# New instruction orders for an audio tower kernel, and other batches in its sorted group

## The chip, the cores and the metric

The kernel runs on one core of a Trainium2 chip. The metric is the device time of one execution in microseconds; the time shown is the median of three. One execution was also recorded by the hardware profiler, and all rows below come from it. A core has a matrix engine (TensorE, PE in the profile), VectorE (DVE), ScalarE (ACT), GpSimd (POOL) and SyncE (SP), which here issues DMAs. Each engine takes its own instructions strictly in order and waits on semaphores that others raise.

## The reference

The input is 8 batches of 375 rows of 128 numbers, all in float32. Each batch passes through three parts:

```python
# token part
h = silu(conv1(x));  h = silu(conv3(h));  h = conv1(h)          # 128 -> 64 -> 64 -> 128
y = layer_norm(h + x);  y = layer_norm(gelu(y @ wf1) @ wf2 + y)
h = max over 3 neighbouring rows of y                            # 373 rows are left
# attention part
n = layernorm(h);  q = (n @ Wq + bq) * s;  k = n @ Wk + bk
h = h + softmax(q @ k.T) @ n
# mixture of 8 experts, the two best of each row
n = layernorm(h);  w = top-2 gates of softmax(relu(n @ gw1) @ gw2)
h = h + sum over e of w[e] * (gelu(n @ we1[e] + be1[e]) @ we2[e] + be2[e])
```

## The kernel before

Batches go through the parts one by one or in pairs. Every step has a short name and a number, and each engine's order is written out by hand as a list of such names (lines 55 to 118). The lists are walked by five loops (TensorE at line 956, VectorE 671, ScalarE 513, GpSimd 440, SyncE 366), so the place of a name in a list is the place of its instructions in that engine's queue. In TensorE's list the number behind the colon is the PSUM bank (one of eight) that the step writes; `claim` (line 939) makes the step wait until the last reader of that bank is done. ScalarE and VectorE share the evacuation of PSUM: a name such as `b1` or `pt0` may stand in either list, and the engine in whose list it stands does the copy. Names that also stand in TensorE's list are there the matrix step, and in the other lists what follows it.

The steps, in the order in which data pass them:

- `a1` to `a7`: the token part. `a1` and `a2` are convolutions, each followed by a tanh and an affine copy on ScalarE (1.15 us together) and a product on VectorE. `a3` is the third convolution; VectorE adds the input and takes the statistics of a layer norm. `p1` on GpSimd turns these into a scale (lines 444, 446, and 451 and 453 when the norm is applied by ScalarE), `l1` applies it, `a4` transposes. `a5` and `a6` are the feed-forward part, `p2` and `l2` its norm, `a7` the transposition, `mp` the maximum over three rows.
- `hr`, `p3`, `l3`, `b1`, `bq`, `bk`, `sc0` to `sc2`, `pt0` to `pt2`, `at`: the attention of one batch. VectorE's `sc` is the row maximum, ScalarE's the exponential.
- `p4`, `l4`, `h1`: the norm ahead of the experts and its transposition into `x32`. `g1`, `g2`, `g3` are the gates of a pair of batches.
- Four batches are dense: every expert is computed for every row. `D1.n` is half of a first layer (two matmul instructions at line 1110), `dg` its GELU on ScalarE (line 621), `D2` the second layer (twelve instructions at line 1117), `da` the weighted sum on VectorE (line 871), `ct` and `bd` the biases of the second layers.
- Four batches are sorted: `rk` and `cnt` rank the rows by expert, `scat` (24 indirect DMAs on GpSimd, line 469) writes rows into a sorted buffer in DRAM, `lx` (SyncE) and `lw` (GpSimd, line 479) load 19 blocks of 256 rows and the weights of each block's expert, `T`, `L1`, `L2` on TensorE (lines 1126, 1134, 1143) with `xT`, `gl`, `yv` compute them, `st` stores them, `gat` (24 indirect DMAs, line 491) gathers each row's two results, and `fin` (lines 927 and 931) adds them. Of the sorted buffer's tables (`cnt` on VectorE) every block is known only after the last of the four batches is ranked, and no gather starts before the last block is stored.
- `out` and `od` on SyncE store the results of sorted and dense batches.

Before the change batches 0, 1, 4, 5 are sorted and 2, 3, 6, 7 dense. `GROUPS` (line 25) says so; the number of `D1`, `D2`, `da` counts along the list of dense batches, eight experts each, so that `D1.0` to `D1.31` are batches 2 and 3.

Of the kernel before, what the change touches and what calls it, by code (L numbers as in the profile page):

```python
# [60 lines left out]
sc0.3:0 sc1.3:6 sc2.3:7 at.2:5 hr.4:6 g2.0:0 pt0.3:7 pt1.3:1 pt2.3:2 a4.6:3 a4.7:7 at.3:1 hr.5:3 h1.2:0 a5.3:7
D1.0:0 D1.1:6 b1.4:1 D1.2:2 bq.4:1 bk.4:3 D1.3:5 h1.3:4 D1.4:3 g1.1:4 g2.1:4 sc0.4:1 sc1.4:4 sc2.4:7 rk.0:0
b1.5:6 a6.6:2 bq.5:6 bk.5:0 a6.7:3 sc0.5:0 sc1.5:1 sc2.5:4 pt0.4:7 pt1.4:6 pt2.4:5 D1.5:7 at.4:6 ct.0:0 ct.1:5
pt0.5:4 pt1.5:1 pt2.5:0 bd.0:4 at.5:0 D2.0:4 D1.6:7 D1.7:5 h1.4:6 D2.1:0 D2.2:5 a7.6:2 D2.3:4 h1.5:2 D1.8:0
a7.7:3 g1.2:2 D1.9:4 D1.10:3 g2.2:2 D1.11:0 hr.6:3 D2.4:4 D1.12:3 D1.13:0 D1.14:2 D1.15:5 D2.5:6 D2.6:0 D2.7:5
rk.2:2 cnt.0:3 b1.6:7 D1.16:1 bq.6:7 bk.6:1 D1.17:2 D1.18:1 D1.19:2 D1.20:1 D1.21:2 sc0.6:7 sc1.6:2 sc2.6:4
hr.7:1 bd.1:6 D2.8:3 D1.22:1 D1.23:7 D2.9:2 D2.10:4 D1.24:5 D1.25:7 D1.26:3 D1.27:5 D2.11:2 D1.28:4 D1.29:5
b1.7:3 pt0.6:4 pt1.6:2 pt2.6:5 bq.7:4 at.6:5 T.0:4 bk.7:2 L1.0:4 T.1:3 D2.12:7 L2.0:3 L1.1:2 T.2:3 T.3:7 sc0.7:4
sc1.7:5 L2.1:2 h1.6:7 L1.2:3 T.4:7 L1.3:2 L2.2:3 L1.4:7 L2.3:3 sc2.7:2 L2.4:3 T.5:7 T.6:1 D2.13:0 L1.5:1 T.7:2
pt0.7:5 pt1.7:0 L1.6:3 pt2.7:0 D1.30:5 T.8:2 D1.31:0 D2.14:7 L2.5:3 L2.6:5 L1.7:3 T.9:5 L1.8:0 L2.7:3 T.10:5  # L70
# [1119 lines left out]
```

## Time and profile before

| | us |
|---|---|
| median of 3 runs | 287.95 (287.29 to 288.83) |
| the profiled execution's own time | 289.53 |
| its span, first to last instruction | 287.7 |
| TensorE busy | 248.6 (86%) |
| VectorE busy | 156.2 (54%) |
| ScalarE busy | 160.7 (56%) |
| GpSimd busy | 130.7 (45%) |
| mean granted TensorE clock | 0.955 |

The span is what the trace covers; the execution's own time is 1.8 us longer. An engine is busy while it works on an instruction, not while it waits on a semaphore. The granted clock is 1.0 where TensorE runs at 2.4 GHz and 0.5 where it runs at 1.2 GHz.

### The profile page before, as it was taken

The numbers are of one execution on the slowest core, as the hardware profiler recorded it, in microseconds if no ns is written. First come the engines' busy times: TensorE is split into PE (matmuls) and PEld (weight loads), VectorE is DVE, ScalarE is ACT, GpSimd is POOL, SyncE is SP. The second block draws the span as 40 slices with busy tenths as digits, with TensorE's granted clock in tenths as the row PEclk, the third lists the DMA queues.
The fourth block names the chain that finished last, engine by engine and source line by source line (L and its number), as shares of the span: only waits on it lengthen the run. The fifth ranks groups of instructions, "written<-read, shape, count | busy, mean of one in ns | idle before, by whom it ended". The sixth has DMA issues, their size and how long they took to land.

```text
span 287.7 us, 5162 instructions
## 1 busy us (share of the span) xinstructions
PE 248.6 (86%) x1484; PEld 191.6 (67%) x1484; DVE 156.2 (54%) x646; ACT 160.7 (56%) x333; POOL 130.7 (45%) x225
## 2 busy tenths in 40 slices
...
PEclk9986977999999999995999999999999999999898
...
GB/s 123 186 162 271 326 405 295 0 0 2 1 2 0 2 2 21 45 36 10 0 2 30 48 63 260 245 208 160 186 190 232 26 75 39 45 80 68 66 49 53
DMA packets 22318, 28.87 MB, mean 100 GB/s; under 512 B 5791, under 2 KB 18532, under 8 KB 22292
## 3 DMA queue, kind: packets, MB, share of 16 engines
...
q10 hardware_dynamic: 576, 0.10, 0.2%
q14 instruction: 14, 0.11, 0.1%
...
## 4 chain that ended last, share of the span: by engine, by line
PE 43%; POOL 22%; issue 15%; DVE 7%; DMA 5%; ACT 3%; POOLq 2%; ACTq 1%; DVEq 0%
POOL xs L469 10%; POOL yg L491 9%; PE PS L1143 6%; PE PS L1134 5%; PE PS L970 4%; PE PS L1117 4%; PE PS L1055 3%; PE PS L1037 3%; DMA wm_p<-in_wm 3%; PE PS L1110 3%; PE PS L949 2%; POOL rstd L446 2%; PE PS L1006 2%; PE PS L1007 2%; PE PS L986 2%
## 5 line engine op out<-in xcount | busy, mean ns | idle before, releaser
L621 ACT ACTIVATE gd<-PS,bias 128x373 f32<-128x373 f32 x64 | 35.6, 573 | 29.7 <-PE PS L1110 28.4
L1117 PEld LDWEIGHTS PS<-w_all,gd 128*125 128x125 f32 x384 | 48.5, 201 | 3.8 <-issue 0.6
L1117 PE MATMUL PS<-w_all,gd 128*125 128x128 f32 x384 | 49.4, 286 | 0.0
L1110 PE MATMUL PS<-xt_sb,w_all 128*128 128x373 f32 x128 | 47.0, 488 | 2.7 <-DVE x_sb L871 2.4
L491 POOL DMA_INDIRECT yg<-ys,pos_y x24 | 29.2, 1217 | 25.7 <-issue 25.7
L469 POOL DMA_INDIRECT xs<-xn,pos_x x24 | 28.8, 1199 | 18.6 <-DVE pos_x L844 12.0
L871 DVE SCALAR_TENSOR_TENSOR x_sb<-PS,comb,x_sb 125x128 f32<-125x128 f32 x84 | 24.2, 344 | 20.8 <-PE PS L1117 20.0
L444 POOL TENSOR_TENSOR ve<-mv,eps 125x3 f32<-125x3 f32 x32 | 7.6, 238 | 57.7 <-DVE mv L654 57.6
L1110 PEld LDWEIGHTS PS<-xt_sb,w_all 128*128 128x128 f32 x128 | 21.8, 190 | 14.4 <-issue 6.0
L446 POOL TENSOR_TENSOR rstd<-ve,mhalf 125x3 f32<-125x3 f32 x32 | 27.5, 860 | 2.5
L479 POOL DMA_DIRECT2D blk_w<-w_all x19 | 10.5, 552 | 32.6 <-issue 23.1
L633 ACT ACTIVATE gb_t<-PS,blk_w 128x256 f32<-128x256 f32 x38 | 15.8, 470 | 11.3 <-PE PS L1134 11.2
L1143 PEld LDWEIGHTS PS<-blk_w,gb_t 128*128 128x128 f32 x152 | 18.4, 191 | 3.7 <-ACT gb_t L633 2.6
L1143 PE MATMUL PS<-blk_w,gb_t 128*128 128x128 f32 x152 | 20.3, 280 | 0.5 <-ACT gb_t L633 0.4
L1134 PE MATMUL PS<-xb_t,blk_w 128*128 128x256 f32 x76 | 19.5, 383 | 0.0
L917 DVE TENSOR_TENSOR yblk<-PS,blk_w 128x256 f32<-128x256 f32 x19 | 8.0, 423 | 19.6 <-PE PS L1143 19.4
L1055 PEld LDWEIGHTS PS<-xn,prob_t 125*125 125x125 f32 (+1 forms) x144 | 16.7, 187 | 2.6 <-issue 2.2
L1055 PE MATMUL PS<-xn,prob_t 125*125 125x129 f32 (+1 forms) x144 | 17.7, 276 | 0.7 <-ACT prob_t L594 0.3
L970 PE MATMUL PS<-hc,wm_p 128*128 128x375 f32 x24 | 11.9, 649 | 5.8 <-DMA wm_p<-in_wm 4.9
L1037 PE MATMUL PS<-k_t,q_t 128*125 128x373 f32 x48 | 16.8, 483 | 0.1
L949 PE MATMUL PS<-ident,xn 124*128 124x124 f32 (+1 forms) x48 | 8.4, 289 | 8.0 <-ACT xn L509 7.5
L1134 PEld LDWEIGHTS PS<-xb_t,blk_w 128*128 128x128 f32 x76 | 13.1, 190 | 2.5 <-ACT xb_t L626 0.7
...
## 6 DMA issues: line engine op xcount, KB each, us to landing
...
```

What stands on the lines that cost most here:

```text
L446: pool.tensor_tensor(rstd[i][:, n % 2, :], ve[i][:, n % 2, :], mhalf[:], ALU.pow)\
L469: pool.indirect_dma_start(xs[g], bass.IndirectOffsetOnAxis(ap=pos_x[:, b // 2, s, i:i + 1], axis=0), xn4[:, b % XN4, j, :], None).then_inc ...
L491: pool.indirect_dma_start(yg[:, m % 2, s, j, :], None, ys[g], bass.IndirectOffsetOnAxis(ap=pos_y[:, b // 2, s, i:i + 1], axis=0))\
L621: act.activation(gd[:, k % GD, c, 0:TP], of("D1", n)[:, 0:TP], ACT.Gelu, bias=bias128[:, 2 + k % E * HC + c:3 + k % E * HC + c]).then_inc( ...
L871: last = dve.scalar_tensor_tensor(flat(dst)[j], flat(of("D2", n)[0:P, :])[j], w[:, j, b % 2, e:e + 1], flat(h2[:, b, :])[j], ALU.mult, ALU ...
L970: last = pe.matmul(f[:, 0:T], wm_p[:, k, :], hc1[:, k:k + T], start=(k == 0), stop=(k == 2))
L1037: pe.matmul(f[0:P, 0:TP], q_t[:, s, OFF[j]:OFF[j] + P], k_t[:, s, :], start=True, stop=True)\
L1055: last = pe.matmul(f[0:P, j * (D + 1):(j + 1) * (D + 1)], prob_t[0:ROWS[c], s, c, OFF[j]:OFF[j] + P], xn3[0:ROWS[c], s, c, :], start=(c == ...
L1110: pe.matmul(f[:, 0:TP], w_all[:, k % E, c * 128:(c + 1) * 128], x32[:, DENSE[k // E], 0:TP], start=True, stop=True).then_inc(S["D1"], 1)
L1117: last = pe.matmul(f[0:P, j * D:(j + 1) * D], gd[:, n % GD, c, OFF[j]:OFF[j] + P], w_all[:, n % E, H + c * D:H + (c + 1) * D], start=(c == ...
L1134: last = pe.matmul(f[:, c * BLK:(c + 1) * BLK], blk_w[i][:, c * 128:(c + 1) * 128], xb_t[n % 2][:], start=True, stop=True)
L1143: last = pe.matmul(f[:, t * D:(t + 1) * D], gb_t[n % 2][:, c, t * 128:(t + 1) * 128], blk_w[i][:, H + c * D:H + (c + 1) * D], start=(c == ...
```

## The change

All instructions stay; their orders in the five lists change, TensorE's steps get other banks, and 56 evacuation steps change between ScalarE and VectorE. The sorted batches become 2, 3, 4, 5, the dense ones 0, 1, 6, 7, so `D1.0` to `D1.31` now belong to batches 0 and 1, and `rk.1` and `cw.0` replace `rk.0` and `cw.1`. ScalarE's list goes from 238 to 228 steps, VectorE's from 170 to 180: VectorE takes over five `l1`, three each of `a4`, `l3`, `bk` and `h1`, four `b1`, one `l4`; ScalarE takes over six `a7`, three `bq` and three `pt`, all net. The diff, cut to the places that the prediction speaks of:

```diff
-GROUPS = ((0, 1, 4, 5),)
+GROUPS = ((2, 3, 4, 5),)
...
 PE_ORDER = """
-a1.0:0 a2.0:0 a3.0:0 a1.1:1 a3.1:2 a1.2:2 a2.1:0 bf.0:2 a4.0:1 a2.2:3 a4.1:0 a3.2:1 a1.3:2 a3.3:3 a5.0:0 a6.0:0
-a6.1:3 a4.2:2 a3.4:1 a3.5:4 a4.3:5 a7.0:0 a7.1:3 a5.1:5 a4.4:3 a6.2:5 hr.0:3 hr.1:0 a4.5:4 a6.3:1 a5.2:4 a2.3:0
...
-T.17:7 L1.16:1 D1.35:7 D1.36:3 T.18:2 D1.37:0 L1.17:4 L2.16:2 L1.18:7 L2.17:4 ct.2:3 L2.18:7 ct.3:0 bd.2:3
...
+a1.0:0 a2.0:0 a1.1:1 a3.0:0 a3.1:1 a2.1:2 bf.0:1 a4.0:0 a1.2:3 a1.3:2 a4.1:0 a3.2:1 a3.3:3 a5.0:0 a2.2:2 a6.0:3
+a6.1:2 a4.2:0 a3.4:1 a3.5:4 a4.3:5 a2.3:6 a7.0:3 a7.1:2 a5.1:0 a4.4:2 hr.0:0 hr.1:2 a6.2:6 a6.3:2 a4.5:0 a3.6:3
+a3.7:5 a5.2:0 b1.0:4 bq.0:4 bk.0:3 b1.1:0 a7.2:6 a6.4:1 sc0.0:3 sc1.0:6 sc2.0:2 bq.1:5 bk.1:0 a7.3:4 a6.5:7
...
+pt2.5:1 D1.8:4 D1.9:3 at.5:7 h1.4:4 hr.7:3 D2.4:2 D1.10:4 D1.11:7 D1.12:3 D1.13:4 D1.14:7 D1.15:3 h1.5:4 D2.5:7
...
+L1.17:3 L1.18:4 g2.3:7 L2.17:3 L2.18:4 D2.15:3 D1.32:4 D1.33:7 D1.34:0 D1.35:1 D1.36:5 D1.37:4 ct.2:7 ct.3:0
...
 DVE_ORDER = """
-a1.0 a2.0 a3.0 a3.1 a1.1 a1.2 bf.0 a4.0 a2.1 a3.2 a3.3 a2.2 a6.0 a6.1 a3.4 a3.5 a7.0 a7.1 mp.0 a1.3 a6.2 hr.0
...
-yv.16 yv.17 yv.18 bd.2 da.16 da.17 da.18 da.19 da.20 fin.0 da.21 da.22 da.23 bd.3 fin.1 da.24 da.25 da.26 fin.2
-da.27 da.28 da.29 fin.3 da.30 da.31
+a1.0 a2.0 a1.1 a3.0 a3.1 l1.0 bf.0 l1.1 a2.1 a1.2 a3.2 a3.3 a1.3 a2.2 a6.0 a6.1 a3.4 a3.5 a4.2 a4.3 l1.4 mp.0
...
+yv.12 yv.13 yv.14 yv.15 yv.16 g2.3 yv.17 yv.18 g3.3 cw.3 da.15 bd.2 da.16 bd.3 da.17 da.18 fin.0 da.19 da.20
+da.21 fin.1 da.22 da.23 da.24 da.25 fin.2 da.26 da.27 da.28 fin.3 da.29 da.30 da.31
...
 POOL_ORDER = """
-p4.0 p3.2 p4.1 p3.3 p1.6 p1.7 p4.2 p3.4 p4.3 p3.5 scat.0 scat.1 scat.2 scat.3 scat.4 scat.5 scat.6 scat.7 scat.8
-scat.9 scat.10 p4.4 scat.11 p2.6 p4.5 p2.7 p3.6 scat.12 scat.13 scat.14 scat.15 scat.16 scat.17 scat.18 scat.19
-scat.20 scat.21 scat.22 scat.23 p3.7 lw.0 lw.1 lw.2 lw.3 lw.4 lw.5 p4.6 lw.6 lw.7 lw.8 lw.9 lw.10 lw.11 lw.12
...
+p2.4 p2.5 p4.0 p3.2 p4.1 p2.6 p2.7 p3.3 p4.2 p3.4 p4.3 p3.5 p4.4 scat.0 scat.1 scat.2 scat.3 p4.5 scat.4 scat.5
+scat.6 scat.7 scat.8 scat.9 scat.10 scat.11 p3.6 p3.7 scat.12 scat.13 scat.14 scat.15 scat.16 scat.17 scat.18
+scat.19 scat.20 scat.21 scat.22 scat.23 lw.0 lw.1 lw.2 lw.3 p4.6 p4.7 lw.4 lw.5 lw.6 lw.7 lw.8 lw.9 lw.10 lw.11
```

## Rows read from the trace of the kernel before

**Rows 1.** The page: the span, and the granted clock in 40 slices
```profile
span 287.7 us, 5162 instructions
PEclk9986977999999999995999999999999999999898
```

**Rows 2.** Busy time in stretches: stretch and length, then each engine, PEclk, DMA, GB/s
```profile
16.40:125.20 108.80, 96.80 (x570) 71.71 (x570) 80.69 (x344) 74.92 (x160) 51.47 (x106) 0.94 0.29 100
125.20:135.60 10.40, 6.58 (x33) 6.24 (x32) 2.78 (x9) 5.09 (x12) 7.67 (x16) 0.67 0.08 20
180.00:190.00 10.00, 9.53 (x62) 7.74 (x61) 3.42 (x9) 5.39 (x15) 3.15 (x7) 1.00 0.71 240
177.20:236.30 59.10, 58.57 (x388) 48.95 (x387) 22.49 (x91) 36.41 (x83) 10.96 (x22) 1.00 0.50 173
236.30:281.60 45.30, 41.61 (x259) 33.77 (x256) 22.05 (x75) 15.37 (x27) 29.21 (x24) 0.96 0.23 59
```

**Rows 3.** Timeline of the first 40 us: start, length, engine, instruction, idle before
```profile
11.19 4.09 PE L970 MATMUL PS<-hc,wm_p 128*128 128x375 f32 x6 [4.94 <-DMA wm_p<-in_wm]
18.36 0.85 PE L962 MATMUL PS<-xt_sb,wc_p 128*64 128x375 f32 x4
...
23.30 3.51 PE L970 MATMUL PS<-hc,wm_p 128*128 128x375 f32 x6 [0.26 <-DVE hc L688]
33.76 1.28 ACT L559 ACT_TABLE_LOAD   x1 [0.55 <-PE PS L999]
35.77 0.46 PE L1006 MATMUL PS<-wf_p,f 128*125 128x128 f32 x2 [2.10 <-ACT f L559]
```

**Rows 4.** Timeline of TensorE, 44 to 57 us
```profile
44.60 0.51 PE L949 MATMUL PS<-ident,n 125*128 125x125 f32 x3 [1.57 <-ACT n L509]
...
56.70 0.88 PE L949 MATMUL PS<-ident,xn 125*128 125x125 f32 x6
```

**Rows 5.** The chain of waits: start, length, what (two full-rate stretches)
```profile
137.36 0.63 PE PS L1110 x2
...
199.21 1.31 PE PS L1117 x12
```

**Rows 6.** Instruction groups by form: busy, mean ns of one, idle before
```profile
L662 DVE TENSOR_SCALAR xn<-h,mv,rstd 125x128 f32<-125x128 f32 x6 | 1.7, 342 | 0.0
L746 DVE TENSOR_SCALAR y_t<-PS,cols 128x375 f32<-128x375 f32 x6 | 3.9, 664 | 2.3 <-PE PS L949 2.3
L766 DVE TENSOR_SCALAR q_t<-PS,bias 128x373 f32<-128x373 f32 x6 | 3.6, 605 | 2.6 <-PE PS L1027 1.5 <-DVE w_top L847 0.7 <-DVE mv L654 0.4
```

**Rows 7.** Timeline of ScalarE, 61 to 64 us
```profile
61.94 1.28 ACT L588 ACT_TABLE_LOAD   x1
63.24 1.03 ACT L588 ACTIVATE prob<-PS,nmax 125x373 f32<-125x373 f32 x2
```

**Rows 8.** Timeline of several engines, 124 to 131 us
```profile
124.84 0.31 DVE L654 BATCH_NORM_AGGREGATE mv<-stat 125x2 f32<-125x6 f32 x3
...
126.52 0.89 POOL L446 TENSOR_TENSOR rstd<-ve,mhalf 125x3 f32<-125x3 f32 x1
...
128.05 1.26 ACT L509 ACTIVATE xn<-x_sb,nmr,rstd 125x128 f32<-125x128 f32 x3 [5.35 <-POOL nmr L453]
...
129.37 0.88 PE L949 MATMUL PS<-ident,xn 125*128 125x125 f32 x3 [3.83 <-ACT xn L509]
```

**Rows 9.** Timeline of TensorE at 172 us, and of POOL and SP before it
```profile
168.13 1.19 POOL L469 DMA_INDIRECT xs<-xn,pos_x  x1 [0.30 <-issue]
172.43 9.70 SPq L376 DMA_DIRECT2D blk_x<-xs  x7
...
172.50 0.54 PE L949 MATMUL PS<-ident,xn 125*128 125x125 f32 x3 [1.64 <-ACT xn L509]
```

**Rows 10.** Timeline of TensorE at 264 us
```profile
264.22 2.07 PE L1110 MATMUL PS<-xt_sb,w_all 128*128 128x373 f32 x4 [2.38 <-DVE x_sb L871]
...
277.50 2.79 PE L1117 MATMUL PS<-w_all,gd 128*125 128x128 f32 x24
```

**Rows 11.** The chain of waits, last 52 us: start, length, what
```profile
236.30 0.44 DVE yblk L917
...
239.53 1.29 POOL yg L491
...
274.55 3.47 DMA yg<-ys,pos_y
278.04 0.89 DVE acc L927 x3
```

More of the change, by code:

```diff
@@ L61 @@
[L61 to L70, printed above, removed]
@@ new lines @@
+at.1:2 hr.3:7 a7.4:6 a7.5:1 a6.6:0 h1.0:4 a6.7:6 b1.2:2 D1.0:4 D1.1:7 D1.2:1 h1.1:3 bq.2:2 bk.2:4 g1.0:7 D1.3:2
+sc0.2:4 sc1.2:7 b1.3:2 sc2.2:1 g2.0:0 bq.3:2 bk.3:3 a7.6:0 D1.4:2 sc0.3:3 sc1.3:0 pt0.2:1 pt1.2:7 pt2.2:4
+sc2.3:5 D1.5:7 at.2:4 pt0.3:5 hr.4:6 pt1.3:0 pt2.3:3 ct.0:5 ct.1:1 a7.7:0 at.3:3 bd.0:1 bd.1:0 h1.2:6 hr.5:5
+D2.0:4 b1.4:5 D2.1:2 bq.4:5 h1.3:7 bk.4:3 D1.6:5 g1.1:1 sc0.4:3 sc1.4:4 b1.5:2 g2.1:1 sc2.4:5 bq.5:2 bk.5:3
+D1.7:4 pt0.4:5 sc0.5:3 sc1.5:2 sc2.5:5 pt1.4:1 pt2.4:0 D2.2:7 at.4:1 rk.1:3 hr.6:7 D2.3:2 pt0.5:5 pt1.5:0
```

67 lines of the change are left out of this document (35 added, 32 removed).

## The prediction
> **What bounds the kernel now.** I read the page first, then busy time by stretches, then the timeline around each idle stretch of TensorE, and the chain of waits for the end. TensorE is the engine to follow: from 177 to 236 us it is busy 58.6 of 59.1 us [rows 2]. Its work at full rate is fixed: a `D1` takes 0.63 us and a `D2` 1.31 us [rows 5], so 0.11 us for one small matmul instruction. Only four things can move the span: idle time of TensorE, its half-rate stretches, what is placed behind the last sorted block, and the fixed end. The reader is to see these stalls:
> - In the head TensorE waits for weights until 11.2 us, then for ScalarE and VectorE between convolutions (11.2, 23.3, 35.8) [rows 3], then for layer norms (44.6) [rows 4]. The clock row shows reduced slices there [rows 1].
> - At 125.5 TensorE stands 3.8 us for batch 4's norm: its statistics were ready at 125.15, but GpSimd was inside a row of `scat` and got to the power at 126.5, ScalarE to `l4` at 128.05 [rows 8]. Behind the stall the granted clock is low, 0.67 over 10.4 us, and twelve `D2` instructions take twice 1.31 us. A clock at 1.2 instead of 2.4 GHz over some 6 us makes about 2.7 us more.
> - At 170.9 it stands 1.6 us for batch 7's `l3` [rows 9], whose `p3` is queued behind the last `scat`.
> - At 261.8 it stands 2.4 us for a bank that `da` frees late [rows 10], because VectorE sat in a `fin`; again the half rate follows (four `D1` instructions in 2.07 us).
> The end is two chains side by side. `L2.18` ends at 236.3; store, 24 gathers and their landing bring `fin.3` at 278.0 [rows 11], which is 41.7 us later, then 1.8 us for `fin.3`, 1.8 us for two `da`, and 6.1 us to store: 51.4 us, 287.7. TensorE's last `D2` ends at 280.3 [rows 10], 44 us behind `L2.18`.
>
> **The change part by part,** as shifts of the end of `L2.18` (236.3), and then the end.
>
> *A, what stands ahead of `L2.18`.* Before, 38 `D1` and 16 `D2` and one `ct` stand ahead; after, 32, 15 and none. 6 x 0.63 + 1.31 + 0.33 = 5.4 us earlier. This costs TensorE nothing in total and lets the gathers start earlier: -5.4.
>
> *B, the head.* `a1.1` moves ahead of `a3.0`. It now runs right behind `a2.0` (ends 15.3) and its tanh and copy (1.15 us) follow at 16.4 instead of 19.3; VectorE's product is done near 18.3, and `a2.1` can start at about 19.3 instead of 23.3. `a1.2`, `a1.3` and `a2.2` now fill waits of ScalarE on `a4.0` and `a5.0`. `a5.0` has its table load of 1.28 us and GELU [rows 3] behind it in both orders; following every step by the durations above I get `a6.0` near 31.3 instead of 35.8, with the same steps ahead of it in both lists. Then `a2.3` (2.0 us) is moved ahead of `a7.0`, where it covers the norms' waits [rows 4], and `a4.2`, `a4.3` on VectorE let `a5.1` go. Continued to `b1.0`, I get 48 instead of 56.7 us with equal work ahead. The hand count has no semaphore hops and may not see a lost clock stretch. I take -7.0; bounds -9 (the hand count) and -2 (only half of the first gain survives). The inputs of batches 6 and 7 are needed 4 us sooner; the `xb` steps on them ran before 27.7 us, so they are in by then.
>
> *C, the middle, until VectorE has batch 5's statistics.* This is at 125.2 before. Ahead of `at.5` TensorE gets four `D2`, four `D1`, two `a7`, `bd.1` and `hr.6` more: 5.2 + 2.5 + 0.7 + 0.7 + 0.3 = 9.4 us. They are not new work, they come from later, and fill waits; with B the same point is 125.2 + 9.4 - 7.0 = 127.6. But VectorE's load grows: between 16.4 and 125.2 it is busy 80.7 of 108.8 us, 74% [rows 2]. It gains ahead of this point five `l1`, three `l3`, one `l4` (0.87 each, from three at 0.342 that overlap), `l2` twice, four `a4` (0.66), `bk`, `bq`, `h1`, `b1`, `pt` (0.55 to 0.61), `mp.3`, four `da` (0.9), `bd.1`, `hr.6`: 25.7 us, and gives away five `a7`, three `bq`, five `pt`, `l2`, `l4`, `l3`, `a4`: 11.4 us (sizes from [rows 6]). So 95.0 us of work in 111.2 us, 85%. It can hold that only if it seldom waits, so I add 3.0 us of new stalls; bounds 0 and 10 (where it would be 78%). ScalarE has four more table loads here, at `sc0.2`, `sc0.4`, `sc0.5` and the returns to `dg`: 5.1 us, less 2.8 us of steps given away, 77 us of 74.9 before: it is not last. C: +3.0.
>
> A page bears on the table loads. The row shows 1.28 us and the exponential 0.02 us behind it [rows 7]. The Trainium skill, "ScalarE: Activation LUTs", section "What ACT_TABLE_LOAD costs", says that a drain of about 1.38 us comes on top, 2.66 us a switch. By that rule the four switches would cost ScalarE 10.6 us instead of 5.1, and C would be nearer its upper bound; the row contradicts it here, so nothing is taken from it.
>
> *D, the stall at 125.5.* `p4.4` now stands ahead of `scat.0` and `p4.5` behind only four `scat`, and `h1.4` has `hr.6`, `pt.5`, `D1.8`, `D1.9` and `at.5` between it and `at.4`. The norm's 3.8 us wait goes, and the 2.7 us of half rate with it: -6.6. What is late next is `rk.2` and, right behind it on VectorE, `l3.6`, `l3.7` and `b1.6`, where TensorE has only `cnt`, `D1.23` and `D2.9` as cover: some 0.5 us each for four places, +2.0; bounds 0 and 6.6 (another stall with its own slow clock). D: -4.6.
>
> *E, the stall at 170.9.* `p3.7` now goes ahead of `scat.12`: -1.6, with a short wait for a copy, -1.8 in all. The price of that place: 12 `scat` start one power later. Is the sorted stage then late? `scat` at 1.5 us each: 12 from `rk.2`'s positions take 18 us, the last lands 4.3 us after its start, then `lx.0` (before: 168.1 to 172.4 [rows 9], and 2.4 us to land). Behind `rk.2` the new list has 25.7 us of TensorE work ahead of `T.0`, against 2 + 16.5 + 4.3 + 2.4 = 25.2 us of this chain. It is just covered, with nothing left over.
>
> *F, the sorted stage.* Before, nineteen blocks share 59 us with 25 other steps; after, with six others, they take 40.7 us of work, 2.0 us a block. `L1.n+1` mostly has the bank of `L1.n`, so it waits for the two GELUs (2 x 0.47): 0.87 + 1.05 = 1.9 us a round, under 2.0. `lw` takes 1.7 us of GpSimd each; `p4.6` and `p4.7` stand ahead of `lw.4` and hold it until about 5 us behind `T.0`, where `L1.4` comes 10 us behind. The traffic is 577 KB a block (weights, rows in, rows out by the declared shapes), 2.4 us at the 240 GB/s of the densest stretch [rows 2], with six slots of prefetch. I take +1.5; bounds 0 and +7 (19 blocks at 2.4).
>
> *G, the end.* `fin.3` now has three `da` behind it instead of two: 41.7 + 1.8 + 2.8 + 6.1 = 52.4 us, +1.0; bounds 0 and 3. TensorE's own chain there is 32 x 0.63 + 17 x 1.31 + 2 = 44.5 us, with 7.4 us of `da` and store 51.9: as long. The wait at 261.8 goes, since `D2.25` and `D2.28` have a `da` of slack. SyncE's `od.1` behind `st.18` is ready before it is due.
>
> Sum: 236.3 - 5.4 - 7.0 + 3.0 - 4.6 - 1.8 + 1.5 = 222.0; + 52.4 = 274.4 us of span. The profiled execution took 289.53 for a span of 287.7, and the median is 1.6 us below it: 274.4 + 1.8 - 1.6, about 274.6. A difference under 0.5% (1.4 us) can't be told from no change.
>
> **The rivals.**
> *Sorted stage bound by transfers and GELU rounds.* For it: GB/s 240 while only six blocks are prefetched [rows 2], and hardly any filler is left. Against it: the stage before moved 173 GB/s with TensorE 99% busy, and needs 250 now. At 2.4 us a block it costs 5.5 us over my F: 280.
>
> *VectorE becomes the bound of the middle, and the kernel slower.* Place: 16.4 us to batch 5's statistics. If VectorE's busy share stays at 74% with 95.0 us of work, the point is at 16.4 + 128 = 144.4, 16.8 us behind 127.6 instead of 3; that is a span of 288.2, and with one half-rate stretch as in [rows 2] 291. It decides from a share of 74.6%: below it the change loses. For it: every norm, maximum and copy in its list is in order, and a norm there waits for GpSimd's power. Against it: before, VectorE mostly waited for TensorE, not the reverse; by hand it is 92% busy as far as `at.1`.
>
> *It does not change anything.* If head and middle keep their idle time and only A works, TensorE's last `D2` still ends at 280 and the gain is hidden beside it: 286 to 288.
>
> **How the numbers follow.** Forecast 0.60 (its own range 268 to 279); transfers 0.18 (278 to 284); no change 0.10; VectorE 0.12 (287 to 294). The range 267 to 286 leaves out about 0.05 below and 0.14 above. Faster 0.83, same 0.07, slower 0.10.
>
> **What would show it.** Right: `a2.1` starts near 19.3, `a6.0` near 31 to 33, `b1.0` by 51; no TensorE wait of over 2 us between 60 and 180; `L2.18` ends near 222 and `fin.3` starts 41.7 us later; VectorE's share to batch 5's statistics is over 80%. Wrong: a share of 75% or less there; GpSimd waiting with `scat` for positions beyond 2 us after `rk`; blocks 2.3 us apart; a new slice of low clock past 60 us.

## The result, and the profile after

| | before | after |
|---|---|---|
| median of 4 runs, same chip, us | 288.39 (287.29 to 289.76) | 265.21 (263.95 to 270.33) |
| ratio, 95% interval | | 0.918 (0.912 to 0.924) |
| the profiled execution's own time, us | 289.53 | 265.61 |
| its span, us | 287.7 | 263.7 |
| TensorE busy | 248.6 | 240.9 |
| mean granted clock | 0.955 | 0.976 |

The kernel became 8.2% faster, about 23 us. The forecast was 274.6 with a range from 267 to 286: the direction was right, and the time lies below the range. One of the four executions behind 265.21, the one of 270.33, was a slow one: the ratios here and below leave such executions out, the medians keep them.

The page of the changed kernel, which answers to [rows 1]:

```profile
span 263.7 us, 5144 instructions
...
PEclk9996797999999999999999999999999999999998
```

The clock is reduced only in the head and at the very end; the slice with 5 in the middle of [rows 1] has no counterpart.

Busy time in stretches, which answers to [rows 2] (same columns). The first line ends where VectorE has the statistics of batch 5, the next two are the stretch between two blocks of attention and the sorted stage, then the densest ten microseconds of its traffic and the end:

```profile
16.40:123.10 106.70, 101.00 (x637) 77.47 (x636) 92.95 (x390) 77.12 (x157) 43.68 (x95) 0.95 0.28 97
139.00:167.10 28.10, 25.94 (x161) 20.00 (x161) 18.83 (x65) 13.79 (x24) 16.90 (x17) 1.00 0.32 97
167.10:211.60 44.50, 44.50 (x300) 38.84 (x299) 12.27 (x41) 25.66 (x66) 10.66 (x21) 1.00 0.61 209
170.00:180.00 10.00, 10.00 (x70) 8.40 (x69) 2.91 (x9) 6.68 (x19) 3.06 (x5) 1.00 0.73 243
211.60:258.40 46.80, 45.77 (x287) 36.02 (x285) 25.47 (x104) 20.08 (x37) 29.24 (x24) 1.00 0.25 64
```

VectorE did 92.95 us of work in 106.7 us, a share of 87% where it had 74%, and the point came at 123.1 where it had been at 125.2, although TensorE had 9.4 us more ahead of it. In the sorted stage TensorE is busy in all of the 44.5 us, and its blocks come 2.1 us apart (`T.0` at 167.1, `T.18` at 205.1).

The head of the changed kernel, from the timelines of TensorE and ScalarE, which answers to [rows 3] and [rows 4]:

```profile
9.54 0.97 PE L970 MATMUL PS<-hc,wm_p 128*128 128x375 f32 x1 [3.10 <-DMA wm_p<-in_wm]
...
17.42 0.80 PE L970 MATMUL PS<-hc,wm_p 128*128 128x375 f32 x2
...
29.72 1.28 ACT L559 ACT_TABLE_LOAD   x1 [2.02 <-PE PS L999]
31.01 0.57 ACT L559 ACTIVATE f<-PS,bias 128x375 f32<-128x375 f32 x1
...
31.64 0.48 PE L1006 MATMUL PS<-wf_p,f 128*125 128x128 f32 x2
...
50.41 0.43 PE L949 MATMUL PS<-ident,xn 125*128 125x125 f32 x2
```

`a2.1` starts at 17.4 (before 23.3), `a6.0` at 31.6 (35.8), `b1.0` at 50.4 (56.7).

TensorE's waits in the changed kernel between 60 and 180 us (line, what it waited for: sum, number, longest), all of them:

```profile
PE PS L1037 <- DVE x_sb L871: 2.1, 2, 1.4
```

They are at `sc1.6` and `sc2.6`, whose banks a `da` still reads. The stalls of [rows 8] and [rows 9] are gone: `h1.4` runs at 120.7 without a wait, and while GpSimd works on the next norm's power (124.15) TensorE has dense steps (it is busy 10.32 of the 10.4 us from 123.1):

```profile
120.70 0.48 PE L949 MATMUL PS<-ident,xn 125*128 125x125 f32 x3
...
122.78 0.32 DVE L654 BATCH_NORM_AGGREGATE mv<-stat 125x2 f32<-125x6 f32 x3
124.15 0.89 POOL L446 TENSOR_TENSOR rstd<-ve,mhalf 125x3 f32<-125x3 f32 x1
...
126.92 0.54 PE L949 MATMUL PS<-ident,xn 125*128 125x125 f32 x3
```

The chain of waits of the changed kernel, its shares and its end; it answers to [rows 11]:

```profile
PE 83%; SPq 5%; DVE 4%; DMA 3%; issue 2%; ACT 1%; another core or an unknown queue 0%; DVEq 0%
...
209.74 1.88 PE PS L1143 x16
211.62 1.32 PE PS L1117 x12
...
254.42 3.96 PE PS L1117 x36
258.38 0.02 issue
258.40 0.35 DVE ob L871
```

`L2.18` ends at 211.6 instead of 236.3. The chain is TensorE's own from there on, and no longer that of the gathers; the two are nearly equally long, as VectorE's timeline shows. The last gather lands 41.8 us behind `L2.18` (before 41.7), and the last `da` starts 5 us later, after waiting 0.45 us for TensorE:

```profile
253.37 0.88 DVE L927 SCALAR_TENSOR_TENSOR acc<-yg,w_top,x_sb 125x128 f32<-125x128 f32 x3 [1.84 <-DMA yg<-ys,pos_y]
...
258.40 0.87 DVE L871 SCALAR_TENSOR_TENSOR ob<-PS,comb,x_sb 125x128 f32<-125x128 f32 x3 [0.45 <-PE PS L1117]
```

**Where the 24.7 us at `L2.18` came from.** For a step of TensorE, call its delay its start less the time that all steps listed ahead of it take at full rate. Between two steps the delay grows by TensorE's waits, by what half rate costs, and by short gaps between matmuls that the profile counts as busy (the 2.8 us of the sorted stage below are such gaps: the clock is 1.00 there and no wait is shown). So kernels with different orders can be compared. The table compares one profile with one profile, and its row B holds what the head's clock happened to be in each.

| stretch | step of the sum | delay grows before | after | forecast change | measured change |
|---|---|---|---|---|---|
| work ahead of `L2.18` | A | | | -5.4 | -5.4 |
| start to `b1.0` | B | 29.0 | 23.0 | -7.0 | -6.0 |
| `b1.0` to `at.5` | C | 8.6 | 2.9 | +3.0 | -5.7 |
| `at.5` to `b1.6` | D | 7.2 | 1.2 | -4.6 | -6.0 |
| `b1.6` to `T.0` | E | 4.2 | 3.0 | -1.8 | -1.2 |
| `T.0` to `L2.18` | F | 3.1 | 2.8 | +1.5 | -0.3 |
| sum | | | | -14.3 | -24.6 |
| `L2.18` to the end | G | 51.4 | 52.1 | +1.0 | +0.7 |

A's figure is the same in both columns because it is counted and not measured. Of the 10.4 us between forecast and result at `L2.18`, 8.7 are in C.

### The profile page after: what moved, and what is told of

The parts are those of the page before. It is cut to its first block, busy times and chain, and to the rows that moved or that the text cites. A ratio compares the mean times of both kernels' runs of the same rounds, so it can differ in the third digit from the quotient of the medians.

```text
span 263.7 us, 5144 instructions
## 1 busy us (share of the span) xinstructions
PE 240.9 (91%) x1484; PEld 186.6 (71%) x1484; DVE 163.3 (62%) x671; ACT 151.2 (57%) x307; POOL 126.2 (48%) x207
## 4 chain that ended last, share of the span: by engine, by line
PE 83%; SPq 5%; DVE 4%; DMA 3%; issue 2%; ACT 1%; another core or an unknown queue 0%; DVEq 0%
PE PS L1117 16%; PE PS L1110 14%; PE PS L1143 7%; PE PS L1134 7%; PE PS L1055 6%; PE PS L1037 5%; PE PS L949 4%; DMA xt_sb<-in_xt 3%; PE PS L1044 3%; PE PS L1006 2%; PE PS L1007 2%; PE PS L1027 2%; PE PS L1031 2%; PE PS L986 2%; SPq L330 2%
## 5 line engine op out<-in xcount | busy, mean ns | idle before, releaser
L1110 PE MATMUL PS<-xt_sb,w_all 128*128 128x373 f32 x128 | 45.7, 485 | 0.7 <-DVE x_sb L871 0.6
L1117 PEld LDWEIGHTS PS<-w_all,gd 128*125 128x125 f32 x384 | 44.4, 187 | 2.5
L1117 PE MATMUL PS<-w_all,gd 128*125 128x128 f32 x384 | 45.8, 273 | 0.0
L444 POOL TENSOR_TENSOR ve<-mv,eps 125x3 f32<-125x3 f32 x32 | 6.3, 196 | 63.6 <-DVE mv L654 63.4
L479 POOL DMA_DIRECT2D blk_w<-w_all x19 | 10.4, 550 | 23.3 <-issue 15.6
L1037 PE MATMUL PS<-k_t,q_t 128*125 128x373 f32 x48 | 17.4, 486 | 2.1 <-DVE x_sb L871 2.1
L1055 PE MATMUL PS<-xn,prob_t 125*125 125x129 f32 (+1 forms) x144 | 17.4, 274 | 0.1
L588 ACT ACTIVATE prob<-PS,nmax 125x373 f32<-125x373 f32 x24 | 12.6, 573 | 2.1 <-DVE nmax L772 1.9
L1037 PEld LDWEIGHTS PS<-k_t,q_t 128*125 128x125 f32 x48 | 8.0, 187 | 7.6 <-issue 4.5
```

The source lines that it names most:

```text
L1037: pe.matmul(f[0:P, 0:TP], q_t[:, s, OFF[j]:OFF[j] + P], k_t[:, s, :], start=True, stop=True)\
L1055: last = pe.matmul(f[0:P, j * (D + 1):(j + 1) * (D + 1)], prob_t[0:ROWS[c], s, c, OFF[j]:OFF[j] + P], xn3[0:ROWS[c], s, c, :], start=(c == ...
L1110: pe.matmul(f[:, 0:TP], w_all[:, k % E, c * 128:(c + 1) * 128], x32[:, DENSE[k // E], 0:TP], start=True, stop=True).then_inc(S["D1"], 1)
L1117: last = pe.matmul(f[0:P, j * D:(j + 1) * D], gd[:, n % GD, c, OFF[j]:OFF[j] + P], w_all[:, n % E, H + c * D:H + (c + 1) * D], start=(c == ...
```

## The experiments

All times are medians in us; the ratio is to the kernel before on the same chip, with its interval. Changes of ratio times 288 give the differences below. "Middle" is from the start of `sc0.0` to the start of `at.5`, in the profiled execution. What stands as added on VectorE is the busy time that the page has more than the changed kernel's (163.3 us); the expectations had put it at 4.3 and 13 us.

| kernel | what | time | ratio | middle |
|---|---|---|---|---|
| before | | 288.4 | 1 | 60.3 |
| after | | 265.2 | 0.918 (0.912 to 0.924) | 63.7 |
| a_again | after, once more | 264.8 | 0.919 (0.914 to 0.924) | 63.8 |
| a_oldhead | old order of the first steps | 265.0 | 0.923 (0.918 to 0.929) | 63.9 |
| a_nofill | dense matmuls out of the middle | 272.5 | 0.948 (0.941 to 0.954) | 63.7 |
| a_olddiv | old division of engines | 275.3 | 0.960 (0.953 to 0.966) | 71.0 |
| a_both | both of these | 286.4 | 0.989 (0.982 to 0.996) | 67.0 |
| b_newdiv | before, new division | 310.2 | 1.085 (1.078 to 1.092) | 75.1 |
| a_dve4 | + 3.5 us on VectorE | 263.0 | 0.921 (0.915 to 0.927) | 65.3 |
| a_dve13 | + 11.5 us on VectorE | 275.1 | 0.957 (0.951 to 0.963) | 70.6 |
| a_act3 | + 2.9 us on ScalarE | 264.1 | 0.916 (0.906 to 0.926) | 64.3 |
| b_p4 | before, `p4.4` earlier | 288.2 | 1.005 (1.001 to 1.008) | 62.3 |
| a_oldp4 | `p4.4`, `p4.5` late | 283.4 | 0.979 (0.973 to 0.985) | 63.7 |
| a_late | seven dense steps ahead of `L2.18` | 275.4 | 0.952 (0.946 to 0.958) | 63.8 |
| a_banks | two other banks | 261.1 | 0.913 (0.907 to 0.918) | 63.7 |
| a_banks2 | and two `da` later | 266.6 | 0.915 (0.910 to 0.921) | 63.7 |
| a_best | and three more moves | 263.7 | 0.918 (0.913 to 0.924) | 63.8 |

### The head: a_oldhead

```diff
-a1.0:0 a2.0:0 a1.1:1 a3.0:0 a3.1:1 a2.1:2 bf.0:1 a4.0:0 a1.2:3 a1.3:2 a4.1:0 a3.2:1 a3.3:3 a5.0:0 a2.2:2 a6.0:3
+a1.0:0 a2.0:0 a3.0:0 a1.1:1 a3.1:2 a1.2:2 a2.1:0 bf.0:2 a4.0:1 a2.2:3 a4.1:0 a3.2:1 a1.3:2 a3.3:3 a5.0:0 a6.0:3
```

> The kernel after with the head of before: the same steps up to a5.0 and a2.2 in the old order, banks and division on TensorE, ScalarE and VectorE, all behind them as after. Theory of step B (the head gains some 4 us for everything behind): a6.0 starts 4 us later and the time is 4 to 5 us more, 269 to 270. Rival (the middle is paced by VectorE's work and takes the head's gain in): under 1.5 us more, 265 to 267.

`a2.1` started at 22.1, 4.7 us later than in the changed kernel, but `a6.0` only 1.3 us later, and `b1.0` 1.4 us later (51.8). Even that is within what one head does by itself: in the ten profiles of kernels with the changed head `a6.0` came between 30.2 and 33.3 and `b1.0` between 47.4 and 52.2. The time is 0.5% longer by the ratios, 1.4 us, with intervals that overlap. The rival held. So the move of `a1.1`, on which most of my step B rested, is worth about 1.4 us or less. B's size was right, its reason was not. What makes the rest of the head shorter is not shown: it is not the division, since a_olddiv has `b1.0` at 48.8, and part is the execution's, since b_p4 has the head of the kernel before and its `b1.0` came at 54.5 instead of 56.7. The order behind `a5.0` is what is left, and no run puts it back alone.

### The dense matmuls in the middle: a_nofill

```diff
-at.1:2 hr.3:7 a7.4:6 a7.5:1 a6.6:0 h1.0:4 a6.7:6 b1.2:2 D1.0:4 D1.1:7 D1.2:1 h1.1:3 bq.2:2 bk.2:4 g1.0:7 D1.3:2
+at.1:2 hr.3:7 a7.4:6 a7.5:1 a6.6:0 h1.0:4 a6.7:6 b1.2:2 h1.1:3 bq.2:2 bk.2:4 g1.0:7 sc0.2:4 sc1.2:7 b1.3:2
...
+rk.1:3 hr.6:7 pt0.5:5 pt1.5:0 pt2.5:1 at.5:7 D1.0:3 D1.1:4 D1.2:2 D1.3:6 D2.0:3 D1.4:4 D1.5:5 D2.1:2 D1.6:6
```

> The kernel after with the first ten D1 and four D2 (and their dg and da) taken out of the attention of batches 2 to 5 and put behind at.5 as one block. Theory V (VectorE's own work paces the middle, and the dense matmuls fill TensorE's waits): at.5 ends only 3 to 4 us sooner although 9.4 us of matmuls are gone ahead of it, and the time is 5 to 6 us more, 270 to 272. Rival N (the new lists leave no waits there, with or without filler): at.5 ends 9 us sooner and the time stays within 1.5 us of 265.

This is the run that explains the miss. Ten `D1` and four `D2`, 10 x 0.63 + 4 x 1.31 = 11.5 us of TensorE, left the middle, and the middle stayed at 63.7 us. Busy time between `sc0.0` and `at.5`, one fence for each kernel (columns as before), first the kernel before:

```profile
60.40:120.70 60.30, 55.94 (x348) 41.79 (x346) 49.27 (x222) 45.88 (x99) 24.55 (x48) 1.00 0.03 8
```

the changed kernel:

```profile
54.90:118.60 63.70, 63.57 (x412) 49.16 (x411) 57.04 (x248) 51.75 (x106) 17.78 (x43) 1.00 0.00 1
```

a_nofill:

```profile
55.50:119.20 63.70, 56.80 (x345) 41.73 (x343) 53.42 (x232) 43.41 (x94) 16.73 (x42) 0.95 0.00 1
```

In the changed kernel TensorE is busy 63.57 of 63.70 us. Without the dense steps the stretch still takes 63.70 us, and TensorE waits in short pieces. One reservation: a_nofill's granted clock is 0.95 here, and this profiled execution took 274.97 us, 2.4 more than its median, so in an undisturbed one the middle may be some 2 to 3 us shorter. The chain of attention steps through the engines thus takes 61 to 64 us in this order, and TensorE's work has been filled up to that or a little above. Of the 11.5 us at least 8.5 were free there; outside the middle they are paid, and the kernel loses 3.0%, 8.5 us. Rival N is excluded. Theory V had the right side, but too little of it (3 to 4 us sooner, 5 to 6 us lost), and its reason isn't quite met: VectorE is busy only 53.42 of the 63.70 us, so it is the chain and not VectorE's work alone that takes this time.

### The division of engines: a_olddiv, b_newdiv

The 56 evacuation steps go back to the engine that had them before (a_olddiv), or 55 of them go to the new engine in the order of before (b_newdiv). The steps that don't change engines keep their order; the others are put in where the profile shows them to start. The first lines of VectorE's list, a_olddiv against the changed kernel:

```diff
-a1.0 a2.0 a1.1 a3.0 a3.1 l1.0 bf.0 l1.1 a2.1 a1.2 a3.2 a3.3 a1.3 a2.2 a6.0 a6.1 a3.4 a3.5 a4.2 a4.3 l1.4 mp.0
+a1.0 a2.0 a1.1 a3.0 a3.1 bf.0 a2.1 a4.0 a1.2 a3.2 a3.3 a1.3 a2.2 a6.0 a6.1 a3.4 a3.5 a7.0 a7.1 mp.0 a2.3 hr.0
```

> The kernel after with the 56 evacuation steps back on the engine that had them before, each put in where the profile shows it to start. Theory (the new division is what made the middle 8 us shorter than I forecast): 6 to 9 us more, 271 to 274. Rival (the division hardly matters; order and dense filler do it): within 2 us of 265.

> The kernel before with 55 of the 56 evacuation steps on the engine that has them after, orders otherwise as before. If the division by itself is worth what a_olddiv lost (8 to 10 us): 277 to 280. Rival (order and division only work together, the moved steps are in the way of others here): no gain or slower, 286 to 292.

The old division costs the changed kernel 4.2%, 12 us, of which 7.3 in the middle and 2.8 just before it, from `b1.0` to `sc0.0`. In the middle it isn't a matter of load. Busy time there in a_olddiv:

```profile
56.10:127.10 71.00, 65.58 (x413) 49.38 (x411) 55.37 (x241) 52.70 (x109) 18.37 (x46) 1.00 0.01 1
```

VectorE has 1.7 us less than in the changed kernel and ScalarE 1.0 us more, in 7.3 us more of time. What changed is which step stands in front of which in each queue, and how long single steps take. A norm that ScalarE applies takes 1.26 us instead of VectorE's 0.87 and needs two more short steps on GpSimd before it; GpSimd has 18 steps more in a_olddiv (225 to 207), so that is nine norms, but only three steps more in the middle (46 to 43). No run separates the two. The new division in the order of before costs 8.5%, 24 us more: `b1.0` comes at 61.7 instead of 56.7, and the middle is 14.8 us longer, with 3.9 us more work on VectorE, 3.0 less on ScalarE and a granted clock of 0.95:

```profile
65.40:140.50 75.10, 60.48 (x348) 43.92 (x347) 53.12 (x233) 42.85 (x92) 25.67 (x45) 0.95 0.03 8
```

So a division has no worth that holds in both orders. The places of the moved steps weren't tuned in either run: the 24 us say what a misfit costs and not that no good order exists, and of the 12 us of a_olddiv too a part may be the places and not the engines.

### Do the two gains add: a_both

The edits of a_nofill and a_olddiv together.

> The changed kernel with both edits of a_olddiv (the 56 evacuation steps back on their old engines) and a_nofill (D1.0 to D1.9, D2.0 to D2.3, dg and da behind at.5) at once. It asks whether the 64 us from sc0.0 to at.5 are a chain of steps whose length the division sets, with the dense matmuls lying in TensorE's waits. Theory (chain alone): sc0.0 to at.5 takes 71 us as in a_olddiv (71.0), although 9.4 us of matmuls are gone, and the time is the sum of both losses, 265 + 10 + 7.5 = 282 to 283 us. Rival (the two losses overlap, because the old engines are late only where the dense matmuls' own evacuations stand between the steps): sc0.0 to at.5 falls back to 62 to 65 us, and the time is 273 to 276 us.

```profile
56.80:123.80 67.00, 54.88 (x344) 40.72 (x342) 51.70 (x225) 44.64 (x99) 17.39 (x44) 1.00 0.00 1
```

In the whole time they add: 0.918 + 0.030 + 0.042 = 0.990, measured 0.989. In the middle neither theory is right: it takes 67.0 us, between 63.7 and 71.0. With the old division the chain without the dense matmuls takes 67.0 us at full clock, 3 to 6 us more than with the new one, and 11.5 us of dense matmuls lengthen it by 4.0 us. So 7.5 us of the filler are free with the old division too. What this kernel still has over the kernel before, the new grouping, order and banks, is worth 1.1% (0.4 to 1.8), 3 us. Taken out of the changed kernel, then, the filler is worth 3.0% of its 8.2, the division 4.2, and what is left 1.1. This is a split of the changed kernel and not a list of gains that could be had one by one: b_newdiv shows that the division put in first loses. And no run tests the new grouping by itself, nor the order or the banks.

### How near VectorE is to being the bound: a_dve4, a_dve13, a_act3

The added work is unused: statistics of the layer norm taken again in `at.0` to `at.5`, once (a_dve4) or three times (a_dve13, shown below), and on ScalarE a copy in each of `hr.0` to `hr.5` (a_act3, below it).

```diff
 def ln_stats(i, n, src):
+                if i == 3 and n < 6:
+                    for r in range(3):
+                        for j in range(NJ):
+                            dve.bn_stats(spare[:, r, n, j, :], src[j])
...
+                    if n < 6:
+                        act.activation(ob[:, n, :], of("hr", n)[0:P, 0:NJ * D], ACT.Copy)
```

> The kernel after with three more statistics instructions (0.7 us, results unused) on VectorE in each at.0 to at.5: 4.3 us more work on VectorE in the middle, nothing else. Theory V (VectorE's work paces the middle): at.5 starts 3.5 to 4.3 us later; the waits of 1.4 us at sc1.6 and sc2.6 take a part in, as with the old head, so 2 to 3 us more in all, 267 to 268. Rival (TensorE paces it, VectorE has slack between its steps): at.5 under 1 us later, 265 to 266.

> The changed kernel with about 13 us of unused statistics work added to VectorE in at.0 to at.5 (three times what a_dve4 added, which cost 1.6 of its 4.3 us between sc0.0 and at.5). Theory (the middle is a chain through all engines, in which VectorE has little left: it was at 87% there): the first 4 us are partly absorbed and the rest is paid in full, sc0.0 to at.5 grows by 8 to 11 us to 72 to 75 us, and the time by the same, to 273 to 276 us. Rival (VectorE's work is no bound at all, the slope of a_dve4 goes on): plus 4 to 5 us, sc0.0 to at.5 68 to 69 us and the time 269 to 270 us.

> The kernel after with one more copy (0.48 us, result unused) on ScalarE ahead of each hr.0 to hr.5: 2.9 us more work on ScalarE in the middle. Theory V: ScalarE has room, at.5 starts under 1 us later, 265 to 266. Rival (all in-order engines are tied, any added step costs its length): at.5 2 to 3 us later, 266 to 267.

Busy time in the middle of a_dve4:

```profile
51.90:117.20 65.30, 64.15 (x413) 49.38 (x411) 59.36 (x261) 52.07 (x106) 17.73 (x44) 1.00 0.01 2
```

and of a_dve13:

```profile
56.70:127.30 70.60, 65.74 (x412) 51.01 (x411) 64.89 (x289) 52.75 (x106) 16.86 (x42) 0.98 0.01 1
```

VectorE's busy time in this stretch rises from 57.04 to 59.36 and 64.89 us, the stretch from 63.7 to 65.3 and 70.6. The first 2.3 us cost 1.6, the next 5.5 cost 5.3. The share goes from 89.5 to 90.9 and 91.9%: it hardly rises any more. In a_dve4 the 1.6 us lie between what the theory (3.5 to 4.3) and the rival (under 1) said, and the time shows nothing of them (0.921 against 0.918). From a_dve4 to a_dve13 VectorE's page has 8.0 us more, and the time is 3.6%, 10 us, longer. The middle of a_dve13 is shorter than the 72 to 75 us expected, since the added work was less than 13 us and not all of it lies there, but the time of 275.1 is in the theory's range, and the rival's 269 to 270 is excluded. 2.9 us on ScalarE cost 0.6 us in the middle and nothing that the time shows.

### Where `p4.4` stands: b_p4, a_oldp4

```diff
-p4.0 p3.2 p4.1 p3.3 p1.6 p1.7 p4.2 p3.4 p4.3 p3.5 scat.0 scat.1 scat.2 scat.3 scat.4 scat.5 scat.6 scat.7 scat.8
-scat.9 scat.10 p4.4 scat.11 p2.6 p4.5 p2.7 p3.6 scat.12 scat.13 scat.14 scat.15 scat.16 scat.17 scat.18 scat.19
+p4.0 p3.2 p4.1 p3.3 p1.6 p1.7 p4.2 p3.4 p4.3 p3.5 scat.0 scat.1 scat.2 scat.3 scat.4 scat.5 scat.6 scat.7 p4.4
+scat.8 scat.9 scat.10 scat.11 p2.6 p4.5 p2.7 p3.6 scat.12 scat.13 scat.14 scat.15 scat.16 scat.17 scat.18
...
-p2.4 p2.5 p4.0 p3.2 p4.1 p2.6 p2.7 p3.3 p4.2 p3.4 p4.3 p3.5 p4.4 scat.0 scat.1 scat.2 scat.3 p4.5 scat.4 scat.5
+p2.4 p2.5 p4.0 p3.2 p4.1 p2.6 p2.7 p3.3 p4.2 p3.4 p4.3 p3.5 scat.0 scat.1 scat.2 scat.3 scat.4 scat.5 scat.6
+scat.7 scat.8 scat.9 scat.10 p4.4 scat.11 p4.5 p3.6 p3.7 scat.12 scat.13 scat.14 scat.15 scat.16 scat.17 scat.18
```

> The kernel before with one name moved: p4.4 on GpSimd from behind scat.10 to behind scat.7. Theory of step D (TensorE's 3.8 us wait at 125.5 and the half-rate stretch behind it, 2.7 us, both come from batch 4's norm queued behind scat): the wait goes, TensorE shows full clock from 60 us on, 6.6 us less, 281 to 282 us. Rival (another wait takes its place, since the sorted chain and the gathers set the end): under 2 us less, 286 to 288.

> The kernel after with the places of p4.4 and p4.5 on GpSimd as before: behind scat.10 and scat.11. In the kernel before this place cost a wait of 3.8 us, yet b_p4, which took it away, was no faster. Theory (after has no such reserve: h1.4 and l4.4 stand right behind at.5, and VectorE itself waits for the power): scat.10 ends 16.5 us behind scat.0, TensorE stands 10 to 16 us at h1.4, 275 to 282. Rival (as with b_p4, the place costs nothing): 264 to 267.

In the kernel before the stall of [rows 8] can be removed and nothing is gained. The timeline of TensorE in b_p4 shows `h1.4` at 125.1 without a wait:

```profile
122.58 1.47 PE L1117 MATMUL PS<-w_all,gd 128*125 128x128 f32 x12
123.89 1.42 PE L1110 MATMUL PS<-xt_sb,w_all 128*128 128x373 f32 x4
125.14 0.49 PE L949 MATMUL PS<-ident,xn 125*128 125x125 f32 x3
```

In this profile `L2.18` comes 4.7 us earlier than before, of which 2.2 are already there at `b1.0` and so not the edit's. Between `b1.0` and `L2.18` the stretch around the old stall takes 4.4 us less, but the middle before it takes 2.0 us more (three new short waits stand there, for a `pt`, a `bd` and `at.5` itself, 1.8 us together). Behind `L2.18` another 1.8 us go, 1.6 of them to one more wait for a bank that `da` frees. Over all runs the time isn't shorter; the rival held. In the changed kernel the same place for `p4.4` makes a wait four times as long as the one in the kernel before. GpSimd and TensorE in a_oldp4:

```profile
118.14 1.32 POOL L469 DMA_INDIRECT xs<-xn,pos_x  x1 [15.56 <-DVE pos_x L844]
119.76 1.20 POOL L469 DMA_INDIRECT xs<-xn,pos_x  x1 [0.30 <-issue]
...
133.19 1.18 POOL L469 DMA_INDIRECT xs<-xn,pos_x  x1 [0.30 <-issue]
134.40 0.20 POOL L444 TENSOR_TENSOR ve<-mv,eps 125x3 f32<-125x3 f32 x1
...
136.51 0.88 PE L949 MATMUL PS<-ident,xn 125*128 125x125 f32 x3 [15.43 <-DVE xn L662]
```

The first `scat` needs the positions of the rows that `rk.1` ranks, and those come at 118 us here. Eleven `scat` of 1.5 us stand ahead of the norm's power, and TensorE waits 15.4 us, as the theory said; the kernel loses 6.1%, 18 us, and ends 1 us above its range. Before, those positions came earlier, and the same place cost 3.8 us of wait. The new place of `p4.4` belongs to the new order; it is no gain that can be had alone.

### What stands behind `L2.18`: a_late

```diff
-L2.6:7 L2.7:3 L1.8:7 T.10:3 L1.9:0 T.11:4 L2.8:7 L2.9:0 L1.10:7 T.12:0 L1.11:4 T.13:3 L2.10:7 L1.12:4 T.14:7
-L2.11:3 L1.13:4 T.15:3 L2.12:7 L1.14:4 T.16:7 L2.13:3 L1.15:4 T.17:3 L2.14:7 L1.16:4 T.18:7 L2.15:3 L2.16:4
-L1.17:3 L1.18:4 g2.3:7 L2.17:3 L2.18:4 D2.15:3 D1.32:4 D1.33:7 D1.34:0 D1.35:1 D1.36:5 D1.37:4 ct.2:7 ct.3:0
+L2.6:7 L2.7:3 L1.8:7 T.10:3 L1.9:0 T.11:4 L2.8:7 L2.9:0 D2.15:6 D1.32:1 D1.33:2 L1.10:7 T.12:0 L1.11:4 T.13:3
+L2.10:7 L1.12:4 T.14:7 L2.11:3 D1.34:5 D1.35:1 L1.13:4 T.15:3 L2.12:7 L1.14:4 T.16:7 L2.13:3 D1.36:2 D1.37:6
+L1.15:4 T.17:3 L2.14:7 L1.16:4 T.18:7 L2.15:3 L2.16:4 L1.17:3 L1.18:4 g2.3:7 L2.17:3 L2.18:4 ct.2:7 ct.3:0
```

> The kernel after with D2.15 and D1.32 to D1.37 (5.1 us of matmuls) taken from behind L2.18 and put among L2.9 to L2.14, with their dg and da. Theory of step A (two chains run side by side behind L2.18, and the gathers' is the longer once L2.18 is late): L2.18 ends 5 us later, fin.3 starts 41.8 us behind it, and the time is 4 to 5 us more, 269 to 270. Rival (TensorE's work alone sets the end): within 1 us of the yardstick.

The kernel lost 3.4%, 10 us, twice what step A said. But the seven steps covered something where they stood: `ct.2` now comes right behind `L2.18` and waits for the gates, and the clock row shows reduced slices behind it. Among the blocks, two `L1` now wait for a GELU of ScalarE, which has the `dg` of the moved steps in front of it (the first line is from the list of waits):

```profile
PE PS L1134 <- ACT gb_t L633: 3.0, 2, 1.5
...
221.29 1.26 PE L1096 MATMUL PS<-ident,comb 125*8 125x125 f32 x6 [4.04 <-DVE comb L857]
...
PEclk9979999999999999999999999999999975999999
```

So this run doesn't test A alone. The profile of a_again, the changed kernel once more, has the same head (`b1.0` at 47.7 in a_again, 47.8 here), so the two can be compared: `L2.18` ends at 217.3 and not 209.0, which is 5.1 us of moved matmuls and 3.2 of waits and gaps. Behind it TensorE has 5.1 us less to do and still takes 3.0 us longer to `D2.31`, 50.5 and not 47.5: the 4.0 us at `ct.2`, and a granted clock of 0.90 where a_again had 1.00. The chain that ends last is TensorE's here as well, and `fin.3` (260.85) waits for no gather but stands behind a `da`. The loss is thus waits and half rate on TensorE's own chain, 3.2 + 8.1 = 11.3 us in these two profiles, and not the later gathers that the theory named. Neither it nor the rival held, and whether the gathers' earlier start is worth A's 5.4 us isn't shown by any run.

### A better version: a_again, a_banks, a_banks2, a_best

```diff
-D2.13:1 sc0.6:0 sc1.6:3 sc2.6:1 sc0.7:7 sc1.7:4 sc2.7:2 D1.28:0 D1.29:3 pt0.6:1 D1.30:7 pt1.6:4 pt2.6:1 pt0.7:2
+D2.13:1 sc0.6:0 sc1.6:5 sc2.6:6 sc0.7:7 sc1.7:4 sc2.7:2 D1.28:0 D1.29:3 pt0.6:1 D1.30:7 pt1.6:4 pt2.6:1 pt0.7:2
...
-g2.2 da.6 g3.2 da.7 rk.2 l3.6 l3.7 b1.6 da.8 da.9 da.10 b1.7 cnt.0 da.11 bk.6 da.12 da.13 sc0.6 sc1.6 sc2.6
+g2.2 da.6 g3.2 da.7 rk.2 l3.6 l3.7 b1.6 da.8 da.9 da.10 b1.7 bk.6 cnt.0 da.11 sc0.6 sc1.6 sc2.6 da.12 da.13
```

The first pair of lines is a_banks; a_banks2 also moves `da.12` and `da.13`; a_best also moves `bk.6`, and `D2.12` and `D2.13` behind `sc2.6`.

> The kernel after, unchanged, timed again on the same chip as the next three, as their yardstick: 264 to 266. The granted clock of the first 60 us differs from execution to execution; its profile shows how many half-rate stretches fall there this time.

> The kernel after with two banks changed: sc1.6 from 3 to 5 and sc2.6 from 1 to 6, so that they no longer wait for da.12 and da.13. Theory (TensorE is the bound from there on): the waits of 0.7 and 1.4 us go and the time is 1.5 to 2 us less, 263 to 264. Rival (VectorE reads sc0.6 only after da.13 anyway, the next step waits instead): no change, 265.

> The kernel after with the two banks of a_banks, and on VectorE da.12 and da.13 moved from ahead of sc0.6 to behind sc2.6. In a_banks the wait had moved on: D1.28 stood 1.4 us for bank 0, whose reader is the exponential of sc0.6 on ScalarE, which waits for VectorE's maximum behind da.13. Theory: the maximum comes 1.7 us sooner, the wait goes, in all 3 to 3.5 us less than the yardstick, 261 to 262. Rival (a_banks was a luckier clock, TensorE's waits here cost nothing): within 1 us of the yardstick.

> A version that is to beat both kernels: the changed kernel with sc1.6 on bank 5 and sc2.6 on bank 6 (as a_banks), D2.12 and D2.13 moved behind sc2.6 on TensorE, bk.6 ahead of cnt.0 and da.12, da.13 behind sc2.6 on VectorE. Theory: the waits of 0.7 us at sc1.6 and 1.4 us at sc2.6 go and D1.28 has no new one over 1 us: 1.5 to 2.5 us below the changed kernel, 262 to 263 us. Rival: as in a_banks2 another wait takes their place, or the 1.2 to 2.4 GHz changes in the head hide it: no difference from the changed kernel that can be told, 264 to 266 us.

The wait at `sc1.6` and `sc2.6` went each time, and others came (two of 0.7 and 0.6 us in a_best, one of 2.3 us in a_banks2). In a_banks:

```profile
PE PS L1110 <- ACT prob L588: 1.4, 1, 1.4
```

That is `D1.28`, for the bank that the exponential of `sc0.6` reads. a_banks has the lowest median, but its ratio and that of the unchanged a_again overlap (0.907 to 0.918 and 0.914 to 0.924), and the two versions that go further are at 0.915 and 0.918. None can be told from the changed kernel; a_best's delay at `L2.18` is 0.6 us below a_again's. No version that is surely faster was found.

## Why the prediction was wrong

**The step that failed is C.** It said: the moved matmuls "are not new work, they come from later, and fill waits; with B the same point is 125.2 + 9.4 - 7.0 = 127.6", and then "I add 3.0 us of new stalls". Here is the fault: work that fills waits doesn't push the point back, yet I added its 9.4 us in full. In the sum for `L2.18`, where moved work counts the same at either place, this means that a term is missing: the waits that get filled were put at nothing, and only new stalls were counted. Before, TensorE's delay grew by 8.6 us from `b1.0` to `at.5`; those were the waits to be filled. After, it grew by 2.9. So 5.7 of the 9.4 us took no time, and no new stalls came: 8.7 us against the forecast. The point came at 123.1 instead of my 130.6. a_nofill shows it directly: 11.5 us of dense matmuls in or out change the middle by 3 us at most.

**Why C's bounds didn't hold it.** They were 0 and +10, with nothing below 0. I bounded the stalls that VectorE could add and never the waits that the new order and division could take away. a_olddiv shows what the division takes away: 7.3 us in the middle. I had costed it as load on VectorE alone.

**VectorE as the bound.** Its load was well counted (95.0 us forecast, 92.95 measured), and its share rose to 87%, where the rival needed it to stay at 74%. The reason I gave for it, that VectorE had mostly waited for TensorE, fits this, but no run tests it. And a_dve13 shows how near the rival's mechanism is: from a_dve4 on, 5.5 us more on VectorE in the middle made the middle 5.3 us longer.

**B** was -7.0 and came to -6.0, and its first link held: `a2.1` even came 1.9 us before the forecast 19.3, `a6.0` at 31.6 within 31 to 33. The reason was wrong for most of it: by a_oldhead the early `a2.1` is worth 1.3 us at `a6.0`. The size is one profile's; the mean of the ten with this head has `b1.0` 0.7 us earlier, at 49.7.

**D** (-4.6, measured -6.0): the wait and the half rate behind it went, as said. Of the 2.0 us that I added for what is late next, 0.6 are to be seen. The step's reasoning treats the place of `p4.4` as a gain in itself, which b_p4 contradicts: the same stall removed in the kernel before shortens its own stretch by 4.4 us and the time by nothing.

**E** (-1.8, measured -1.2): GpSimd's last `scat` started at 157.2, and the load of the first block's rows was issued at 162.15 and takes 2.6 us to land by the page, so they were there some 2.3 us before `T.0` at 167.1: more slack than my "nothing left over". The wait at `sc1.6` and `sc2.6`, 2.1 us, was not in the sum.

**F** (+1.5, measured -0.3): the rival of transfers and GELU rounds is excluded. In the densest ten microseconds the traffic was 243 GB/s, and TensorE was busy in all ten. My upper bound, 2.4 us a block, took the 240 GB/s of [rows 2] for a limit; the stage as a whole ran at 209 GB/s, its blocks came 2.1 us apart and not the 2.3 that I had named as a sign of being wrong, and TensorE never waited for a block. The work of the stage is 41.7 us by the table above (44.5 less 2.8) and not the 40.7 I wrote, a slip that the sum doesn't use.

**G** (+1.0, measured +0.7) was as worked out. **A** is the matmuls' own time; a_late was to test it and didn't, so its -5.4 is counted and not shown. I said that TensorE's chain behind `L2.18` would be as long as that of the gathers; it is now the one that ends last.

The table load: [rows 7] had 1.28 us with the exponential 0.02 us behind it, and in the changed kernel the GELU at 31.01 starts 0.01 us behind a load of 1.28 us. The drain of 1.38 us that the Trainium skill ("ScalarE: Activation LUTs", section "What ACT_TABLE_LOAD costs") puts on top is not seen here either.
